# A split fp32 second GEMM: the parts of h for two steps in one tile, w2's one step ahead

## What is computed

```
W = weights[condition]                        # one 64x64 matrix per sample
a = einsum('bct,bcd->bdt', x, W)              # x is 32 x 64 x 1024 fp32
h = gelu(einsum('bsd,df->bsf', a, w1) + b1)   # w1 is 1024 x 4096, tanh gelu
out = x + einsum('bsf,fd->bsd', h, w2) + b2   # w2 is 4096 x 1024
```

## Time and profile before

| | us |
|---|---|
| median of 3 runs | 1158.93 |
| the profiled execution's own time | 1159.22 |
| its span, first to last instruction | 1157.4 |
| TensorE matmul busy | 1152.4 |
| VectorE busy | 870.2 |
| ScalarE busy | 561.8 |
| GpSimd busy | 94.7 |

### The profile page before, as it was taken

The page is one execution under the profiler, slowest core; times in us unless marked ns, Lnnn a source line. Parts: engine busy times, 40 slices in busy tenths (PEclk is TensorE's granted clock), DMA queues, the critical chain, the costliest instruction groups (busy, mean ns, idle before and its releaser), DMA issues.

```text
span 1157.4 us, 15233 instructions
## 1 busy us (share of the span) xinstructions
PE 1152.4 (100%) x5468; PEld 1012.7 (87%) x5468; DVE 870.2 (75%) x1190; ACT 561.8 (49%) x963; POOL 94.7 (8%) x124
## 2 busy tenths in 40 slices
PE   9999999999999999999999999999999999999999
PEld 8988888888888888888888888888888888888887
DVE  5888787877466666666658689688899687788996
ACT  5855555555444444444445444444444444444443
POOL 3000000000001000110001121103110101101000
PEclk9999999999999999999999999999999999999999
DMA  9687768866996446764399998758963749966663
GB/s 340 202 292 247 236 265 318 280 241 237 383 399 201 133 126 145 200 198 129 96 326 303 364 315 264 222 200 181 224 187 118 193 140 253 301 196 192 200 155 118
DMA packets 118541, 263.96 MB, mean 228 GB/s; under 512 B 9890, under 2 KB 20162, under 8 KB 117058
## 3 DMA queue, kind: packets, MB, share of 16 engines
q1 hardware_dynamic: 103792, 229.14, 56.4%
q0 software_dynamic: 13824, 33.56, 17.2%
q10 hardware_dynamic: 850, 0.28, 0.1%
HBM read 170.67 MB, written 92.27 MB: 227 GB/s over the span
## 4 chain that ended last, share of the span: by engine, by line
PE 99%; DMA 1%; SPq 0%; DVE 0%; issue 0%
PE ps L741 50%; PE ps L757 46%; PE ps L704 1%; PE ps L689 1%; DMA x<-in_x_dram 1%; PE ps L776 0%; SPq L457 0%; SPq L458 0%; SPq L455 0%; DVE out L1331 0%
## 5 line engine op out<-in xcount | busy, mean ns | idle before, releaser
L741 PE MATMUL ps<-y,lhs 128*128 128x512 f32 x2688 | 581.6, 379 | 0.0
L741 PEld LDWEIGHTS ps<-y,lhs 128*128 128x128 f32 x2688 | 507.6, 189 | 71.8
L757 PE MATMUL ps<-rhs,lhs 128*128 128x512 f32 x2472 | 533.7, 379 | 0.0
L757 PEld LDWEIGHTS ps<-rhs,lhs 128*128 128x128 f32 x2472 | 467.2, 189 | 66.3
L939 ACT ACTIVATE lhs<-h_raw 128x512 fp32r<-128x512 f32 x208 | 131.0, 630 | 295.9 <-PE ps L757 283.0
L1167 DVE TENSOR_TENSOR lhs<-h_raw,lhs 128x512 fp32r<-128x512 f32 x208 | 143.8, 691 | 98.2 <-ACT lhs L939 98.2
L1033 DVE TENSOR_TENSOR lhs<-w_raw,lhs 128x512 fp32r<-128x512 f32 x128 | 88.5, 692 | 103.5 <-ACT lhs L840 102.0
L840 ACT ACTIVATE lhs<-w_raw 128x512 fp32r<-128x512 f32 x128 | 80.5, 630 | 163.0 <-PE ps L741 161.4
L1170 DVE TENSOR_TENSOR rhs<-w_buf,rhs 128x512 fp32r<-128x512 f32 x208 | 142.3, 684 | 0.0
L944 ACT ACTIVATE rhs<-w_buf 128x512 fp32r<-128x512 f32 x208 | 128.5, 618 | 0.0
L1033 DVE TENSOR_TENSOR lhs<-s_w,lhs 128x512 fp32r<-128x512 f32 x96 | 66.3, 691 | 68.2 <-ACT lhs L840 66.4
(11 more groups left out here) (56 smaller groups left out, 425.0 us busy)
## 6 DMA issues: line engine op xcount, KB each, us to landing
h_raw<-p_mem SPq DMA_DIRECT2D x80, 512.0 KB, 5.5
w_raw<-in_L_ffn_inter_w_dram SPq DMA_DIRECT2D x27, 1024.0 KB, 7.9
p_mem<-part SPq DMA_DIRECT2D x96, 256.0 KB, 6.8
w_buf<-in_L_ffn_output_w_dram SPq DMA_DIRECT2D x12, 2048.0 KB, 16.6
h_raw<-q_mem POOLq DMA_DIRECT2D x32, 512.0 KB, 7.6
y_mem<-y_out SPq DMA_DIRECT2D x28, 512.0 KB, 4.3
y<-y_mem SPq DMA_DIRECT2D x7, 2048.0 KB, 12.7
q_mem<-part SPq DMA_DIRECT2D x56, 256.0 KB, 6.9
```

Source lines behind the costliest of these rows:

```text
L741: last = nc.tensor.matmul(ps[:, bank, :], w[:, k, :], by_pairs(y[i][:, part, k, :]), start=(i in FRESH and k == 0 and u == 0), stop=(k == ...
L757: last = nc.tensor.matmul(ps[:, bank2(t, tb), :], lhs[s % RING][:, a, blk(tb)], by_pairs(rhs[r][:, w, :]), start=(t in FRESH2 and q == 0 a ...
```

## The change

The second GEMM's lhs tiles become two tiles of 8 KB a partition, each with both parts of two steps. One copy of ScalarE and one subtraction of VectorE (128x1024) make a pair. The rhs ring shrinks to two tiles; the very last step has a third tile, `rhs_end`, at another place. w2's parts for step m + 1 may be begun when TensorE starts step m, where they had been begun for step m + 2. The pair n may be begun when TensorE starts step 2n - 2. In the lists of ScalarE and VectorE, the place for step m now holds w2's part for m + 1, then (m even) the h pair that begins at m + 2, then, in the last group's leftovers, those for m + 1, and then `beside` for m. That `beside` stood behind the parts of step m + 2 before. `load_h` waits for the pair's subtraction. The first GEMM is as before.

```diff
-        rhs = [at(f"rhs{i}", 172 + 4 * i, [2, BANK], F32R) for i in range(RING)]
+        lhs_pair = [at(f"lhs_pair{i}", 160 + 8 * i, [2, 2, BANK], F32R) for i in range(2)]
+        rhs = [at(f"rhs{i}", 176 + 4 * i, [2, BANK], F32R) for i in range(2)]
+        rhs_end = at("rhs_end", 200, [2, BANK], F32R)
...
+        def rhs_tile(m):
+            return rhs[m % 2] if m < RANK * KS - 1 else rhs_end
+        def lhs_tile(n):
+            return lhs_pair[(n + 1) % 2]
...
                 if n >= HRING:
-                    sp.wait_ge(lhs_lo, step2(0, 2 * (n - HRING) + 2))
+                    sp.wait_ge(lhs_lo, S1STEPS + n - HRING + 1)
...
             def second(t, q):
-                s, r = step2(t, q), rhs_n(t, q) % RING
-                pe.wait_ge(lhs_lo, s + 1)
+                n, r = rhs_n(t, q) // 2, rhs_tile(rhs_n(t, q))
+                pe.wait_ge(lhs_lo, S1STEPS + n + 1)
                 pe.wait_ge(rhs_lo, rhs_n(t, q) + 1)
...
-            def high2(t, q):
-                s, r, n = step2(t, q), rhs_n(t, q) % RING, rhs_n(t, q) // 2
-                act.wait_ge(step_done, s - RING + 1)
+            def high2(n):
+                act.wait_ge(step_done, S1STEPS + 2 * n - 2)
                 act.wait_ge(h_in[n % HRING], 16 * (n // HRING + 1))
                 if summed(n):
                     act.wait_ge(h_sum[n % HRING], 16 * sums(n))
-                nc.scalar.activation(lhs[s % RING][:, 0, :], h_part(t, q), ACT.Copy).then_inc(lhs_hi, 1)
+                nc.scalar.activation(lhs_tile(n)[:, 0], h_raw[n % HRING][:], ACT.Copy).then_inc(lhs_hi, 1)
+
+            def high2_w2(m):
+                t, q = divmod(m, KS)
+                if 2 <= m < RANK * KS - 1:
+                    act.wait_ge(step_done, S1STEPS + m - 1)
...
-            for t in range(RANK):
-                for q in range(KS):
-                    high2(t, q)
-                    if t == 0:
-                        trail(GROUPS - 1, q)
+            high2(0)
+            high2_w2(0)
+            trail(GROUPS - 1, 0)
+            for m in range(RANK * KS - 1):
+                high2_w2(m + 1)
+                if m % 2 == 0 and m // 2 + 1 < PAIRS:
+                    high2(m // 2 + 1)
+                trail(GROUPS - 1, m + 1)
...
-            for t in range(RANK):
-                for q in range(KS):
-                    low2(t, q)
-                    if t == 0:
-                        trail_second(GROUPS - 1, q)
-                    if t > 0 or q >= 2:
-                        beside(*divmod(rhs_n(t, q) - 2, KS))
+            low2(0)
+            low2_w2(0)
+            trail_second(GROUPS - 1, 0)
+            for m in range(RANK * KS - 1):
+                low2_w2(m + 1)
+                if m % 2 == 0 and m // 2 + 1 < PAIRS:
+                    low2(m // 2 + 1)
+                trail_second(GROUPS - 1, m + 1)
+                beside(*divmod(m, KS))
```

More of the change, by code:

```diff
@@ L266, in w2_part @@
             return w2_buf[BUFFER[t]][:, q, :]
-        def h_part(t, q):
-            return h_raw[(t * KS + q) // 2 % HRING][:, q % 2, :]
+        def rhs_tile(m):
+            return rhs[m % 2] if m < RANK * KS - 1 else rhs_end
+        def lhs_tile(n):
+            return lhs_pair[(n + 1) % 2]
         def summed(n):
@@ L756, in second @@
                     for u, (a, w) in enumerate(((0, 0), (0, 1), (1, 0))):
-                        last = nc.tensor.matmul(ps[:, bank2(t, tb), :], lhs[s % RING][:, a, blk(tb)], by_pairs(rhs[r][:, w, :]),
+                        last = nc.tensor.matmul(ps[:, bank2(t, tb), :], lhs_tile(n)[:, a, q % 2, blk(tb)], by_pairs(r[:, w, :]),
                                                 start=(t in FRESH2 and q == 0 and u == 0),
@@ L765, in last_two @@
                 t, q = LAST, KS - 2
-                s, r = step2(t, q), rhs_n(t, q)
-                pe.wait_ge(lhs_lo, s + 2)
+                n, r = rhs_n(t, q) // 2, rhs_n(t, q)
+                pe.wait_ge(lhs_lo, S1STEPS + n + 1)
                 pe.wait_ge(rhs_lo, r + 2)
@@ L775, in last_two @@
                             for u, (a, w) in enumerate(((0, 0), (0, 1), (1, 0))):
-                                last = nc.tensor.matmul(ps[:, bank, cols], lhs[(s + i) % RING][:, a, blk(tb)],
-                                                        by_pairs(rhs[(r + i) % RING][:, w, :])[:, cols.start // 2:cols.stop // 2, :],
+                                last = nc.tensor.matmul(ps[:, bank, cols], lhs_tile(n)[:, a, i, blk(tb)],
+                                                        by_pairs(rhs_tile(r + i)[:, w, :])[:, cols.start // 2:cols.stop // 2, :],
                                                         start=(e == 1 and i == 0 and u == 0),
@@ L943, in high2 @@
                     act.wait_ge(w2_in[BUFFER[t]], {0: 16, 1: 16, 4: 16, 8: 32, 12: 16, 15: 32, 16: 32, 19: 16}[t])
-                nc.scalar.activation(rhs[r][:, 0, :], w2_part(t, q), ACT.Copy).then_inc(rhs_hi, 1)
+                nc.scalar.activation(rhs_tile(m)[:, 0, :], w2_part(t, q), ACT.Copy).then_inc(rhs_hi, 1)
             def y1_high(kb, i):
@@ L1162, in within, with low2, low2_w2 @@
                     add_c11(n, 0)
[L1164 to L1167, removed]
+            def low2(n):
+                dve.wait_ge(lhs_hi, S1STEPS + n + 1)
+                nc.vector.tensor_tensor(lhs_tile(n)[:, 1], h_raw[n % HRING][:], lhs_tile(n)[:, 0].bitcast(F32),
                                         ALU.subtract).then_inc(lhs_lo, 1)
-                dve.wait_ge(rhs_hi, rhs_n(t, q) + 1)
-                nc.vector.tensor_tensor(rhs[r][:, 1, :], w2_part(t, q), rhs[r][:, 0, :].bitcast(F32),
+            def low2_w2(m):
+                dve.wait_ge(rhs_hi, m + 1)
+                nc.vector.tensor_tensor(rhs_tile(m)[:, 1, :], w2_part(*divmod(m, KS)), rhs_tile(m)[:, 0, :].bitcast(F32),
                                         ALU.subtract).then_inc(rhs_lo, 1)
```

## The result

The changed kernel takes 1161.83 us (median of 9 runs, 1160.72 to 1163.72) where the kernel before takes 1158.93 (9 runs beside it, 1158.7 to 1159.5). The ratio is 1.0027, with a 95% interval of 1.0018 to 1.0036: slower by 2.9 us. The forecast was 1160.3, within 0.2% of no change. The time lies inside the stated range (1159.2 to 1162.2), which was wide because of the rivals, and outside the forecast's own range (1160.0 to 1160.6). By the median the likeliest class was the wrong one: 0.27% is on the slow side of the 0.2% line, though the interval reaches down to 0.18%. The runs are also spread over 3 us, where those of before are spread over 0.8.

What follows compares the result with a forecast made beforehand. TensorE at its own pace of 0.2158 us per matmul was taken to bound the kernel. Losses of 0.65 and 0.70 us at the second GEMM's start, other terms 0, gave 1158.93 + 1.34 = 1160.3 us, range 1159.2 to 1162.2.

Steps and rivals of the forecast that it cites:

- the forecast's own range: Whole kernel: 1160.0 to 1160.6 us, from 0.05 to 0.26 hand-over and 0.1 on each 1024 instruction.
- the likeliest class: Whole kernel: same time, within 0.2% (2.3 us) of no change, given 0.74.
- What bounds the kernel: Both GEMMs: TensorE stands at its own 0.2158 us per matmul, so work taken from ScalarE and VectorE buys nothing.
- the rival by which TensorE isn't at its own pace: Matmul stream: lighter load on the memory's ports lets TensorE run quicker, 1150 us; chance 0.03.
- Part 1: h pairs: fewer, larger instructions save 9 us of busy time on each of ScalarE and VectorE; worth 0.
- Part 2: Ordinary steps: w2's tiles one step ahead cost 0; 0.41 us less 0.25 hand-over leaves 0.16 margin.
- Part 4: Start of the second GEMM: VectorE's leftover combinations delay w2's parts, losing 0.65 us before step 4, 0.70 before step 6.
- Its last reading: Step 10 of the second GEMM: despite its late h pair, w2's part is on time with 0.14 us left.
- part 3: VectorE's list and h loads: moved additions cost nothing; h's tile is freed earlier, each load gets 1.6 us more.
- Rival (b): Late h transfers come later still: step 10 waits 1.72 us more, 1162.0 us, or half, 1161.0; chance 0.14.
- the rule of step 10: Late pair at the start: from its landing, ScalarE's copy, VectorE's subtraction, addition and w2's part, set against the due time.
- Rival (c): Ordinary steps: the 0.16 us margin is missing and 73 pairs each lose; 1162.5 or 1167.6 us; chance 0.13.

Runs made afterwards that it cites:

- (9): Kernel after with VectorE's leftovers and product 0's additions and mixes respaced, and 2 MB w2 loads moved behind h pairs 6 and 77: 1159.32 us.
- (10): Kernel after with two extra 128x128 VectorE additions at every even step from step 8 on: 1176.62 us.
- (11): Kernel after with only two 2 MB w2 loads moved, one behind h pair 77, the first one behind h pair 6: 1160.34 us.
- (5): Kernel before, with SyncE's four w2 loads that wait for `rhs_lo` waiting for one part more: 1158.97 us against 1158.99.
- (12): Kernel before, with only the 2 MB w2 load ahead of h pair 77 waiting for two more parts: 1159.06 us against 1159.10.
- 2: Kernel after with one 2 MB w2 load moved from just before the load of h pair 77 to just behind it: 1160.57 us.
- (1): Kernel after with the start's leftovers spread out: one beginning moved a place later, product 0's four mixes moved to steps 10 to 13: 1161.99 us.
- (6): Kernel after with one extra VectorE memset of 128 columns at every even step from step 8 on: 1161.58 us.
- (7): Kernel after with three extra VectorE memsets of 32 columns at every even step from step 8 on: 1162.03 us.

## Why the prediction was right and wrong

- What bounds the kernel: right. TensorE's matmuls keep their 0.2158 us, and no kernel here is faster than before. 9.2 us less of ScalarE's busy time and 4.5 less of VectorE's bought nothing, and the rival by which TensorE isn't at its own pace fell: (9), less its one wait of 0.31, has the 533.70 us of the kernel before for 2472 matmuls. The trace disagrees with the 131 ns that the Trainium skill's page "TensorE: Matmul & The Clock Gate", section "Back-to-back issue gap", states.
- Part 1 (0): right in cost, with the instructions as read from the earlier trace rows. VectorE's saving was 4.5 us and not 9, which costs nothing where it is ahead.
- Part 2 (0, margin 0.16): right, and shown by (10); the margin is 0.25, as the hand-over is 0.15 where 0.25 was taken. A late weight load does start late (2.35 us idle of that queue before step 154, and 0.03 us between its start and the matmul's). No more than 0.15 stands between VectorE's end and the matmul, but the second matmul comes 0.08 late. By the Trainium skill's rule on row groups (the same page, section "The mechanism") the prediction had worked out 0.05; no wait here bears that out.
- Part 4 (1.35): right in place and in size, 0.61 and 0.71 for 0.65 and 0.70, in part by luck: a hand-over taken 0.10 too long stood in for the 0.08 of the second matmul. (11) has it alone, at 1.45 in the median. Its last reading failed: step 10, said to be on time by 0.14, waited 0.20, as its pair was taken 0.5 us later than worked out. The prediction had named a wait there as a sign of being wrong.
- The step that failed is in part 3: "each load gets 1.6 us more. That can only help." I followed h's tiles alone. The pair's load did go out 1.1 us earlier, and its landing came 2.2 later. SyncE's list holds other loads, and one waits for the count that part 2 had just made a step later. But that is the smaller half of it: (5) and (12) show that the late load costs nothing where two steps of lead remain. What I never did was ask of each late pair of the trace before whether the new lead covered it. I asked it of steps 10 and 12, which showed in the window that I read, and not of pair 77 at 1010 us, which waits by 2.19 us in the same list of waits. Worked by the rule of step 10, with the landing at its old time and the step 1.34 us later, it would have had 1.3 us in hand (1010.28 + 4.04 + 0.25 = 1014.57, due 1015.84). That rule is wrong so late in the GEMM, since the pair's load waits for a subtraction that is as late as TensorE. With the landing moved by the same 1.34 the slack is about zero.
- Rival (b), late transfers of h, given 0.14, is what happened: a little of it at step 10, where it was looked for, and most of it at another pair and with another cause. The late landing it feared at step 10 was 0.7 us later, not 2.0, in line with its own argument that the queue is full.
- Rival (c) was rightly low, and its price was wrong: past the margin about half of the pairs pay, each with the 0.08 on top.
- That 1161.83 lies in the stated range is no credit to the sum. The range had room for rival (b), and the 2.21 us at pair 77 stood in no term.

The sum in the median: 1.45 for the start's backlog (11), 0.1 to 0.2 for pairs 5 and 6 (2 against 11), 1.3 for pair 77 (after against 2): 2.9 us.

What stays open: ScalarE takes pair 77 394.6 to 395.1 us after the second GEMM's start in the three profiled kernels with the old lead, and at 396.8 in the kernel after. The load's place explains 0.5 of that. Much of the rest differs between executions: with the same load 1.5 us ahead of the pair, step 154 was late by 0 (1), 1.1 (6), 1.8 (7) and 2.2 us (after), one profile each. What moves the landing from one to the next is not shown. Moving the load behind the pair removed the wait whatever its cause.

## What to carry to other kernels

Cutting the lead of a ring from two steps to one is free only where nothing was late: list every place of the trace before where a feeding engine waited for a transfer, and work out for each whether the shorter lead still covers it, with all that stands in the list behind it. A count that releases tiles may release loads in another queue as well. With no slack left, the spread of a transfer's landing becomes a spread of the kernel's time. A wait that is removed in front of a fixed landing comes back behind it, so mend both or none. And read the weight loads beside the matmuls: waits of 0.2 and 0.3 us left the matmuls in one piece here, and only the weight loads showed them.

## What the runs showed of the hardware that I had not expected

An operand that VectorE finishes reaches TensorE's next matmul 0.14 to 0.15 us after VectorE's end, in the waits before steps 4, 6 and 154 of the kernel after. The second matmul after such a wait comes 0.08 us late too (5.42 us for 24 matmuls, 10.52 for 48 without a wait before them), so that each stop costs 0.23 beyond VectorE's end. A ring's loss past its margin is paid every second turn when the producer is released by the end of the step before: 0.35, 0, 0.35 us. A 512 KB transfer's landing followed its issue only in part, in a stretch with a DMA share of 1.08: the issue began 2.2 us later (621.54 for 619.30 of the earlier trace rows), held SyncE for 2.72 us in place of 3.92 and so ended 1.0 later, and ScalarE took the pair 0.7 later.
